# Gathering h between the scatter rounds of a graph network kernel, and the summed rows later

## What is computed

```python
# third layer
h = x @ W_in2f
Wij = (shifted_softplus(f_ij @ W_f1 + b_f1) @ W_f2 + b_f2) * rcut_ij[:, None]
x_ij = h[idx_j] * Wij
y = segment_sum(x_ij, idx_i)            # idx_i = src, idx_j = dst
x = layernorm(x + shifted_softplus(y @ W_o1 + b_o1) @ W_o2 + b_o2)
# fourth layer, applied twice
mean = segment_sum(x[src], dst) / max(count, 1)
out = mean @ Wl.T + bl + x @ Wr.T
```

## Time and profile before

| what | value |
|---|---|
| median of 3 runs | 2410.17 us (2402.45 to 2412.42) |
| span of the profiled execution | 2409.0 us |
| busy PE / DVE / ACT / POOL | 87% / 83% / 74% / 63% |
| `edges_first` | about 1107 to 1309 us |
| `nodes_alone` | about 1309 to 1710 us |
| `edges_middle` | about 1710 to 2068 us |

### The profile page before, as it was taken

How to read it: one execution, slowest core, us unless ns; L and a number is a source line. 1 busy time by engine, 2 the same in 40 slices (tenths; PEclk the granted TensorE clock), 3 DMA queues, 4 the chain that set the end, 5 groups by cost and what they waited for, 6 DMA issues and landing times. The chain is left out here.

```text
span 2409.0 us, 45629 instructions
## 1 busy us (share of the span) xinstructions
PE 2090.2 (87%) x14016; PEld 1742.8 (72%) x14016; DVE 1990.3 (83%) x2945; ACT 1791.3 (74%) x3691; POOL 1507.2 (63%) x1114
## 2 busy tenths in 40 slices
PE   5999999999997899998997888888599998487564
PEld 4999999999997677775775777776466666365464
DVE  7999999999997566666996899999488888398554
ACT  4889889988896577776775788888599998276221
POOL 6888766777730434431554655777488884688787
PEclk9999999999999899998999899999899999699776
DMA  4666666555665888886885688888377775786653
GB/s 110 146 168 156 156 167 170 162 147 162 183 183 169 222 254 252 257 238 183 201 203 134 139 185 182 203 199 194 96 188 191 192 193 152 160 204 160 170 161 104
DMA packets 322547, 427.40 MB, mean 177 GB/s; under 512 B 113683, under 2 KB 169589, under 8 KB 322308
## 3 DMA queue, kind: packets, MB, share of 16 engines
q1 hardware_dynamic: 210004, 367.20, 53.6%
q0 software_dynamic: 112000, 56.93, 13.9%
q10 hardware_dynamic: 304, 0.36, 0.0%
HBM read 239.24 MB, written 185.90 MB: 176 GB/s over the span
## 5 line engine op out<-in xcount | busy, mean ns | idle before, releaser
L1782 POOL DMA_INDIRECT acc<-combined,first_ x100 | 206.9, 2069 | 186.5 <-DMA acc<-combined,first_ 77.7
L510 PE MATMUL banks<-mats,g_hT 128*125 128x256 f32 x1000 | 260.1, 383 | 0.0
L529 PE MATMUL banks<-mats,g_zT 128*125 128x128 f32 x2000 | 238.8, 273 | 0.0
L529 PEld LDWEIGHTS banks<-mats,g_zT 128*125 128x125 f32 x2000 | 228.1, 188 | 0.0
L844 POOL DMA_INDIRECT gin_xs<-x,from_ x100 | 126.5, 1265 | 162.5 <-DMA x_of_src<-gin_xs 138.5
L510 PEld LDWEIGHTS banks<-mats,g_hT 128*125 128x125 f32 x1000 | 190.2, 190 | 27.6 <-issue 0.4
L1012 DVE TENSOR_TENSOR gin_acc<-gin_acc,gin_qr 125x512 f32<-125x512 f32 x125 | 86.6, 693 | 117.1 <-ACT gin_qr L974 86.3
L590 ACT ACTIVATE g_zT<-banks,cols 128x500 f32<-128x500 f32 x250 | 178.9, 775 | 4.8 <-PE banks L518 4.8
L573 ACT ACTIVATE g_sq<-banks 125x512 f32<-125x512 f32 x250 | 144.6, 590 | 45.1 <-PE banks L510 32.2
L437 POOL DMA_INDIRECT g_xd<-in_x,idx x100 | 124.8, 1248 | 75.3 <-PE banks L544 48.4
L1837 POOL DMA_INDIRECT em_h<-h,from_ x100 | 142.4, 1424 | 43.6 <-issue 25.6
(11 more groups left out here) (408 smaller groups left out, 6613.3 us busy)
## 6 DMA issues: line engine op xcount, KB each, us to landing
acc<-g_zero SPq DMA_DIRECT2D x126, 224.0 KB
x<-g_x SPq DMA_DIRECT2D x125, 224.0 KB
g_x<-in_xT SPq DMA_DIRECT2D x100, 250.0 KB
gin_x<-x SPq DMA_DIRECT2D x50, 448.0 KB
h<-gin_hr SPq DMA_DIRECT2D x50, 448.0 KB
al_h<-h SPq DMA_DIRECT2D x38, 448.0 KB
al_x<-x SPq DMA_DIRECT2D x38, 448.0 KB
out<-al_out SPq DMA_DIRECT2D x38, 448.0 KB
```

Of the source, the lines that this page charges most:

```text
L510: m = nc.tensor.matmul(bank[0:P, 256 * j:256 * j + 256], HT[q % 2][:, c:c + P], K.W1c, start=False, stop=j == 1)
L529: m = nc.tensor.matmul(pO[q % 2][0:P, D * j:D * j + D], ZT[q % 2][:, h, P * j:P * j + P], K.W2[:, h, :], start=False, stop=j == R - 1 and ...
L1782: pool.indirect_dma_start(out=K.acc, out_offset=bass.IndirectOffsetOnAxis(ap=K.first[:, g, r:r + 1], axis=0), in_=CR[:, g, r * D:r * D + D ...
```

## The change

A new helper `h_rows` issues the four gathers that fetch the `h` rows at the sources of one tile into that tile's slot of `combined`. The slot is free once the round that read it has landed, and that is what POOL already waits for before the next round. So each round is now followed by the gathers for the slot of the round before it. `edges_first` runs 10 rounds and 9 times four gathers; the side program of `nodes_alone` runs four gathers, then 15 rounds with 14 times four gathers between them, the last slot's four gathers, and 16 gathers of `acc` rows into `em_y` (the four tiles that held `h` before). The loop of 100 gathers of `acc` is gone. In `edges_middle` the roles are swapped: `turn` reads the slot and waits for no gather, `turn_y` reads `em_y` and waits for it, the gathers of four tiles ahead fetch `acc` rows and wait for `turn_y(k - 4)`, and `apply_c` waits for `turn`. The semaphore of the `h` gathers lives over two phases and is cleared with the second.

The diff (renamings of the same kind left out):

```diff
@@ -1505,7 +1505,7 @@
                               (2, on(n.reduce_c, dve))])
 
 
-def edges_first(nc, K, CR, rounds):
+def edges_first(nc, K, CR, rounds, got_h):
...
@@ -1549,6 +1549,8 @@
                     past(pool, fi, k)
                     past(pool, added, k - 1, 16 * R)
                     sum_round(pool, K, CR, last - k, added)
+                    if k >= 1:
+                        h_rows(pool, K, CR, last - k + 1, got_h)
...
-def sums_and_gather(K, CR, rounds, added, got, ins):
+def h_rows(pool, K, CR, m, got_h):
+
+    for r in range(R):
+        pool.indirect_dma_start(out=CR[:, m, r * D:r * D + D], out_offset=None, in_=K.h,
+                                in_offset=bass.IndirectOffsetOnAxis(ap=K.from_[:, m, r:r + 1], axis=0)).then_inc(got_h, 16)
+
+
+def sums_and_gather(K, CR, rounds, added, got_h, ins):
 
 
     def side(pool):
+        h_rows(pool, K, CR, EG - rounds, got_h)
         for i, k in enumerate(range(rounds, EG)):
             past(pool, added, i - 1, 16 * R)
             sum_round(pool, K, CR, EG - 1 - k, added)
+            if i >= 1:
+                h_rows(pool, K, CR, EG - k, got_h)
         past(pool, added, EG - rounds - 1, 16 * R)
-        for m in range(EG):
-            for r in range(R):
-                pool.indirect_dma_start(out=CR[:, m, r * D:r * D + D], out_offset=None, in_=K.acc,
-                                        in_offset=bass.IndirectOffsetOnAxis(ap=K.from_[:, m, r:r + 1], axis=0)).then_inc(got, 16)
+        h_rows(pool, K, CR, 0, got_h)
         for k in range(4):
             ins.get(pool, k)
-        pool.wait_ge(got, 16 * R * EG)
+        pool.wait_ge(got_h, 16 * R * EG)
 
     def ahead(sp):
         sp.wait_ge(added, 16 * R * (EG - rounds))
...
 
         self.K, self.CR = K, CR
-        self.X, self.XD, self.YD, self.H = sb("x", 2), sb("xd", 3), sb("yd", 3), sb("h", 4)
...
     def get(self, pool, k):
         for r in range(R):
-            pool.indirect_dma_start(out=self.H[k % 4][:, r, :], out_offset=None, in_=self.K.h,
+            pool.indirect_dma_start(out=self.Y[k % 4][:, r, :], out_offset=None, in_=self.K.acc,
                                     in_offset=bass.IndirectOffsetOnAxis(ap=self.K.from_[:, k, r:r + 1], axis=0)).then_inc(self.got[k % 4], 16)
...
@@ -1874,7 +1883,7 @@
             def _(pool):
                 def get(k):
                     if k >= 4:
-                        past(pool, hT, k - 4)
+                        past(pool, yT, k - 4)
                         ins.get(pool, k)
...
             def _(pe):
                 def turn(k):
-                    past_slot(pe, got, k, 16 * R)
                     past(pe, ydt, k - 1)
                     for j in range(R):
-                        m = nc.tensor.transpose(pT[:, P * j:P * j + P], H[k % 4][:, j, :], K.ident[0:P, 0:P])
+                        m = nc.tensor.transpose(pT[:, P * j:P * j + P], ins.slot(k)[:, j, :], K.ident[0:P, 0:P])
                     m.then_inc(hT, 1)
 
                 def turn_y(k):
                     past(pe, bt, k)
-                    for j in range(R):
-                        m = nc.tensor.transpose(pT[:, P * j:P * j + P], ins.Y(k)[:, j, :], K.ident[0:P, 0:P])
+                    past_slot(pe, got, k, 16 * R)
+                    for j in range(R):
+                        m = nc.tensor.transpose(pT[:, P * j:P * j + P], Y[k % 4][:, j, :], K.ident[0:P, 0:P])
...
                 def apply_c(k):
                     past(dve, nc_.root, k)
-                    past(dve, yT, k)
+                    past(dve, hT, k)
                     nc.vector.tensor_tensor(C(k), banked(pC), nc_.times(k), ALU.mult).then_inc(done, 1)
...
-        ROUNDS, PAIRS = 11, NG // 2 - LATE
-        edges_first(nc, K, CR, ROUNDS)
+        ROUNDS, PAIRS = 10, NG // 2 - LATE
+        got_h = K.lasting("h_got", 1)[0]
+        edges_first(nc, K, CR, ROUNDS, got_h)
         K.end_phase()
         ins = Inputs(nc, K, CR, big)
-        side, ahead = sums_and_gather(K, CR, ROUNDS, sem("added"), sem("y_got"), ins)
+        side, ahead = sums_and_gather(K, CR, ROUNDS, sem("added"), got_h, ins)
         nodes_alone(nc, K, out, PAIRS, side, ahead)
+        K.taken.append(got_h)
         K.end_phase()
```

More of the change, by code:

```diff
@@ L1819, in __init__, with slot @@
         self.K, self.CR = K, CR
-        self.X, self.XD, self.YD, self.H = sb("x", 2), sb("xd", 3), sb("yd", 3), sb("h", 4)
+        self.X, self.XD, self.YD, self.Y = sb("x", 2), sb("xd", 3), sb("yd", 3), sb("y", 4)
         self.IV = [ctx.enter_context(nc.sbuf_tensor(f"em_iv{i}", [128, G], F32)) for i in range(3)]
         self.xin, self.din, self.got = K.lasting("em_xin", 2), K.lasting("em_din", 3), K.lasting("em_got", 4)
-    def Y(self, k):
+    def slot(self, k):
         return self.CR[:, k, :].rearrange("p (r d) -> p r d", r=R)
@@ L1851, in sem @@
             return K.sem(f"{name}_{n}")
-        X, H, XD, YD = ins.X, ins.H, ins.XD, ins.YD
+        X, Y, XD, YD = ins.X, ins.Y, ins.XD, ins.YD
         xin, din, got, IV = ins.xin, ins.din, ins.got, ins.IV
@@ L1856, in edges_middle @@
         BT, YT, YTD = sb("bT", [128, G]), sb("yT", [128, G]), sb("ydT", [128, G])
-        A, B, BD, C = sb("a", [P, R, D]), sb("b", [P, R, D], k=3), sb("bd", [P, R, D], k=3), ins.Y
+        A, B, BD, C = sb("a", [P, R, D]), sb("b", [P, R, D], k=3), sb("bd", [P, R, D], k=3), ins.slot
         AB, SP, ABD, SPD = sb("ab", [128, G]), sb("sp", [128, G]), sb("abd", [128, G]), sb("spd", [128, G])
```

## The result

| | before | after |
|---|---|---|
| median, 17 runs each | 2405.75 us (2399.53 to 2415.76) | 2390.35 us (2386.49 to 2400.32) |
| ratio | | 0.9942, interval 0.9931 to 0.9953 |
| span of the profiled execution | 2409.0 us | 2385.8 us |

The change makes the kernel 0.58% faster, 15.4 us between the medians. The device time of the profiled execution after is 1.7 us more than its span.

What follows compares the result with a forecast made beforehand. Bounds: DVE inside nodes_alone, POOL at its end, PE in edges_first, no waiting for gathers in edges_middle. Terms -9.4 + 0.3 + 0.2 = -8.9 us on the 2409.0 span, plus 1.2 to the median, gave 2401.3 us; range 2394 to 2413.

Steps and rivals of the forecast that it cites:

- the release of the barrier behind SP's store: End of nodes_alone: next phase starts 5.2 us behind SP's last store issue, at 1700.9, counted from traffic.
- the level: Starting time of the sum: the three runs' median, 1.2 us above the 2409.0 us span, uncertain by 3 us either side.
- The end of nodes_alone: POOL finishes 100 us before SP's last store, which then releases the barrier: gain 9.4 us, upper bound 10.6.
- rival E: End of nodes_alone: earlier barrier release (1699.7) and faster store drain, together 11 to 13 us, 2397 to 2399; chance 0.12.
- The tail behind POOL: After POOL's last gather, 4.65 us to the next phase, 3.6 of them the gather's landing; also applied to edges_first.
- edges_first: the cost: Ten rounds with nine sets of gathers, period 15.7 to 16.4 us: cost 0, bound 3.4, up to 9 with a second pause.
- Rival A: POOL ends edges_first, a new wait for the one removed: cost 3 to 9 us, 2404.7 to 2410; chance 0.19.
- Rival B: Gathers held up in edges_first, 2.099 us each, period 19.0 us: 18 us net slower, 2428 us; chance 0.07.
- DMA load (C): Load of 0.88 to 0.9 in edges_first and nodes_alone forecast free; rival: up to 26 us net slower, 2436; chance 0.04.
- nodes_alone's POOL side: POOL's 15 rounds with gathers between, 15.9 us each, end at 1597 with three pauses, 100 us before the last store.
- D: Rival: POOL still ends nodes_alone, needing 100 us more there, a period of 22 us; 2410 us; chance 0.03.
- The small costs: Start of nodes_alone +0.3 us (0 to 2), second clearing in edges_middle +0.2 (0 to 1), otherwise edges_middle zero (-1 to +1).

Runs made afterwards that it cites:

- e2: The kernel before with the last 24 of 100 gathers of summed rows in nodes_alone left out; 2386.83 us against 2409.81, ratio 0.9898.
- e7: The kernel before with the last 12 of 100 gathers of summed rows in nodes_alone left out; 2392.08 us against 2403.29, ratio 0.9958.
- e9_padded: The kernel before with three memsets on POOL behind its last gather of nodes_alone and the wait for the gathers; 2413.97 us against 2406.85, ratio 1.0037.
- e3_rounds11: The changed kernel with 11 rounds in edges_first instead of 10, and 14 in nodes_alone; 2406.01 us against 2409.81 of before, ratio 0.9982.
- The second comparison: Both kernels measured again, unchanged: before 2403.29 us and, under a second name, 2404.61; the changed kernel 2391.99, ratio 0.9952.
- e1_swap_only: The changed kernel without gathers between rounds: 11 and 14 rounds, then all 100 gathers of h; 2406.16 us against 2409.81 of before, ratio 0.9979.

## Why the prediction was wrong

Two terms of the sum were mis-sized and a third part has no place in the trace: the release of the barrier behind SP's store (5.2 us taken, 3.66 measured), and the level, the three runs' median that the sum starts from (3 us allowed, 4.4 measured). The mechanism of the gain held.

**What bounded the kernel: right.** DVE inside `nodes_alone`, POOL at its end, PE in `edges_first`, nobody behind the gathers of `edges_middle`. Two edits that only shorten POOL's list (e2, e7) close the boundary.

**The end of nodes_alone: the mechanism right, the size short.** The release passed to SP's store as forecast. The term was sized 9.4 us and measured 11.0, the extra clearing included. The step that failed is the choice of count: I took the traffic in the windows (5.2 us behind SP's last issue) over the issue at the earlier barrier (4.04 us). Measured is 3.66, and 3.50 to 3.68 over seven profiles. Even the upper bound of 10.6 was 0.4 short. The traces say where the 5.2 us were too long. I took the stores as through 2.8 us behind the last issue; in before the last one lands after 3.06 us, but with POOL's gathers gone after 2.4, as rival E had it. From there I took 2.4 us to the next phase, and 1.22 are measured. That 2.4 came from the earlier barrier, where I took the stores as through at 777.3 by the share of traffic; SP leaves its last wait there only at 778.40, 1.3 us before the start at 779.69.

**The tail behind POOL: wrong in its cause.** "The other 3.6 us as the landing of POOL's last gather" fell with e9_padded: behind a memset, with all gathers landed, 4.22 us are left. On the Trainium skill (Perfetto Trace Analysis, "DMA Instruction — SWDGE (GPSIMD)"): its rule, that such an instruction's end is not the transfer's end, agrees with the trace of before, where the landing is 2.17 us behind the end on POOL. But the rule says nothing of a barrier, and the 4.65 against 1.03 us did not show that the barrier waits for the landing alone. The tail that I drew from it for the last gather of `edges_first` is 3.61 us, not 4.65 (e3_rounds11). It did no harm to the term of `nodes_alone`, since the tail was used there as a measured whole.

**edges_first: the cost right, the period short.** Zero was forecast; 201.5 and 201.6 us were measured. But the period is (1283.05 - 1150.81) / 8 = 16.53 us, outside the 15.7 to 16.4. An add took 2.079 us and a gather 1.313 where I had 2.048 and 1.275, which makes 4 x 2.38 + 4 x 1.61 = 15.97, and waits for ACT's copies (2.2 us in all) and one pause of 2.85 us give the rest. By the threshold of 16.0 that should have cost up to 5 us. It did not, because the threshold stood for more than the period: nine periods of 16.0, a pause of 5.89 and a tail of 4.65, 154.5 us from round 1 to the next phase. Measured are 148.0 us from round 1 to POOL's end (1150.81 to 1298.82), the shorter pause included, and a tail of 3.61 (e3_rounds11), together 151.6 us. There were 153.2 (to 1303.98), 1.5 less than I took, for round 1 waited 7.13 us for the landing of round 0. So a pause 3.0 us shorter and a tail 1.0 us shorter made up for longer periods and a later start. That is luck, and 1.6 us are left of the margin. Rival A shows itself with one round more: 13.8 us. Rival B, slow gathers, had the sign of the mean right and the size wrong: the mean gather was 1.313 us and the longest of the 36 was 1.64, not 2.1. That a gather's time varies is in the rows; that it waits for a port, as the prediction read the 2.099 us of the earlier trace rows, no run here shows.

**DMA load (C): fell.** In the rounds of `nodes_alone` the share is 0.89 and DVE works 99.49 of 100 us. In the steady part of `edges_first`, a window of after beside the earlier trace rows:

```profile
1156.00:1163.00 7.00, 7.00 (x47) 5.13 (x46) 6.93 (x20) 5.46 (x12) 6.08 (x4) 1.00 0.86 195
```

PE is still busy 7.00 of 7.00.

**nodes_alone's POOL side: slower than worked out, and harmless.** Rounds are (1557.01 - 1326.66) / 13 = 17.7 us apart, not 15.9: adds at 2.154 and gathers at 1.385 are 16.6 us, pauses and waits the rest. POOL ended at 1603.56 where 1597 was forecast, and as the phase began 4.9 us earlier than before, that is 11.5 us later within it, against 84 us of cover. D fell by the same number.

**The small costs.** The second clearing was put at 0.2 us: the release behind SP takes 3.62 to 3.68 us in the six profiles that have it and 3.50 in e2_before_less, which has one clearing, so some 0.16. The 0.3 for the start of `nodes_alone` can't be seen, since that start scatters by more. `edges_middle` is 314.5 and 314.6 us.

**The sum.** The miss is 2401.3 - 2390.35 = 10.95 us. 4.4 of it are the level: the three runs had their median at 2410.17, seventeen runs have theirs at 2405.75. I had put 3 us to either side for that. 6.5 are the gain, 15.4 against 8.9; of these 2.1 are the boundary: 11.0 with the clearing in it, against 8.9 for the whole sum. The last 4.4 us have no place in the trace and their cause stays open. The second comparison, 11.3 us between medians, does not have them: there the gain is the boundary's 11.0. So the part of the range that failed is its lower end: with E's 11 us as the true size of the mechanism, and the level and scatter of the medians at 4 us each, it should have reached down to some 2391; the measured 2390.35 lies at that edge.

## What to carry to other kernels

Read a phase's end by who is last at the barrier and by how much the second is behind: work taken off the last engine pays exactly down to the next one (here 20.4 to 11.4 to 9.4 us as POOL fell from 10 us behind SP to 0.9 and then ahead of it), and interleaving it into the waits of an engine that waits for its own landings costs nothing as long as the rate fits (here ten rounds; the eleventh cost 13.8 us). Give a barrier's release one price for each kind of last event, read from the engine's own last wait and what follows it, not from shares of traffic in windows. When the effect is 0.5%, the median of three runs has an error that is no longer small against it (4.4 us here, for a gain of 11 to 15), and the range must hold it.

## What the runs showed that I had not expected

- The end of a phase costs by who is last: 1.0 us behind ACT's copy, 3.5 to 3.7 us behind the issue of SP's last store, 4.5 to 4.8 us behind POOL's last gather at the end of `nodes_alone` (3.6 at the end of `edges_first` in e3_rounds11), and 4.2 us behind a memset of POOL.
- In `nodes_alone` POOL's gathers cost more between adds than in a row: 1.385 and 1.371 us in the two profiles of the changed kernel, against 1.275 and 1.274 before. It is not the table that they read: e1_swap_only gathers the same rows of `h` in a row at 1.266. For the adds no such difference is shown: 2.079 and 2.154 us in one profile of the changed kernel, 2.072 and 2.085 in the other, and 2.091 and 2.139 in e1_swap_only, where they stand apart.
- SP's last store lands 0.6 to 0.7 us sooner when POOL no longer gathers beside it (2.4 us behind the issue against 3.1 to 3.2). This is part of the 11.0 us.
- The granted clock behind a phase's start differs from execution to execution with nothing changed. Between two profiles of one kernel the starts of `nodes_alone` and of the late nodes differ by up to 2.6 and 3.1 us, and `edges_first` by 3.4.
